# Attention: queries projected for four tiles of tokens at once, one pair of heads per bank

## The reference, cut to what matters

```python
q, k, v, g = x @ Wq, x @ Wk, x @ Wv, x @ Wg + bg        # x: 1024 x 256, W: 256 x 1024
q, k = elu(q) + 1, elu(k) + 1                           # the "features"
kv   = einsum('nd,ne->de', k, v);  k_sum = k.sum(tokens)
z    = 1 / clip(q . k_sum, 1e-6)
out  = (q * SCALE) @ kv * z * sigmoid(g)
return concat_heads(out) @ Wo                           # 1024 x 256
```

## Time and profile before

| what | value |
|---|---|
| time of three executions | 1814.41, 1815.03, 1819.37 us |
| the profiled execution | 1819.65 us, its span 1817.9 us |
| PE busy over the span | 1771.5 us, 97% |
| DVE, ACT, GpSimd busy | 1395.9, 1003.8, 528.0 us |
| between 85 and 600 us: PE, DVE, ACT busy | 510.08, 386.37, 205.76 us of 515 |

### The profile page before, as it was taken

How to read it: one execution, slowest core, us unless ns; L and a number is a source line. 1 busy time by engine, 2 the same in 40 slices (tenths; PEclk the granted TensorE clock), 3 DMA queues, 4 the chain that set the end, 5 groups by cost and what they waited for, 6 DMA issues and landing times. The chain is left out here.

```text
span 1817.9 us, 52839 instructions
## 1 busy us (share of the span) xinstructions
PE 1771.5 (97%) x19744; PEld 1554.0 (85%) x19744; DVE 1395.9 (77%) x4325; ACT 1003.8 (55%) x2481; POOL 528.0 (29%) x382
## 2 busy tenths in 40 slices
PE   8999999999999989999999999999999999989998
PEld 7879889889888778888888888888888888888887
DVE  5877877877867788888888687767888888877774
ACT  4443443443434478888887444337777777743333
POOL 0000000000000256666666000016666666611111
PEclk9999999999999999999999999999999999999999
DMA  9200000000020111111111200002111111110011
GB/s 330 83 1 2 2 1 2 1 1 2 1 72 2 40 41 29 26 29 26 29 27 35 100 12 12 1 1 70 28 27 29 27 26 29 32 35 12 6 66 33
DMA packets 64830, 60.44 MB, mean 33 GB/s; under 512 B 16415, under 2 KB 59211, under 8 KB 64718
## 3 DMA queue, kind: packets, MB, share of 16 engines
q1 hardware_dynamic: 64718, 58.88, 10.9%
HBM read 33.95 MB, written 8.39 MB: 23 GB/s over the span
## 5 line engine op out<-in xcount | busy, mean ns | idle before, releaser
L1317 ACT ACTIVATE l_probs<-l_probs,l_negmax 128x192 f32<-128x192 f32 x512 | 225.8, 442 | 86.6 <-DVE l_negmax L1424 86.6
L1142 POOL TENSOR_TENSOR l_t<-l_t,l_rnorm 128x512 f32<-128x512 f32 x128 | 136.1, 1083 | 245.5 <-DVE l_rnorm L1096 245.5
L1264 POOL TENSOR_TENSOR l_probs<-l_probs,l_rowinv 128x768 f32<-128x768 f32 x128 | 185.1, 1466 | 20.1 <-DVE l_rowinv L1453 20.1
L117 PE MATMUL ps<-local_w_hi,l_xT 128*128 128x512 f32 x384 | 158.0, 412 | 1.6 <-PEq L1719 1.1
L1272 POOL TENSOR_TENSOR l_t<-l_t,l_t 128x1024 f32<-128x1024 f32 x62 | 146.9, 2370 | 30.0 <-DVE l_t L1110 18.4
L118 PE MATMUL ps<-local_w_lo,l_xT 128*128 128x512 f32 x384 | 151.6, 395 | 0.0
L119 PE MATMUL ps<-local_w_hi,l_xT 128*128 128x512 f32 x384 | 151.3, 394 | 0.0
L117 PE MATMUL ps<-m_hnT_hi,ffn_w_hi 128*128 128x512 f32 (+1 forms) x352 | 141.0, 400 | 0.0
L512 ACT ACTIVATE attn_exp<-ps 128x512 f32<-128x512 f32 x128 | 76.4, 599 | 116.1 <-PE ps L119 116.1
L119 PE MATMUL ps<-m_hnT_hi,ffn_w_lo 128*128 128x512 f32 (+1 forms) x352 | 138.5, 394 | 0.0
L118 PE MATMUL ps<-m_hnT_lo,ffn_w_hi 128*128 128x512 f32 (+1 forms) x352 | 138.4, 393 | 0.0
(11 more groups left out here) (273 smaller groups left out, 5709.1 us busy)
## 6 DMA issues: line engine op xcount, KB each, us to landing
l_edge<-l_v SPq DMA_DIRECT2D x252, 64.0 KB, 2.0
tok_x<-x SPq DMA_DIRECT2D x16, 512.0 KB, 8.0
shifted<-x SPq DMA_DIRECT2D x64, 64.0 KB, 1.5
m_shifted<-shifted SPq DMA_DIRECT2D x16, 256.0 KB, 2.8
out<-x SPq DMA_DIRECT2D x8, 512.0 KB, 3.2
ffn_w_raw<-ffn_w SPq DMA_DIRECT2D x6, 640.0 KB
local_w_raw<-ffn_wqkv SPq DMA_DIRECT2D x4, 768.0 KB, 5.2
tok_base<-attn_base SPq DMA_DIRECT2D x4, 512.0 KB, 9.0
```

Source lines behind the costliest of these rows:

```text
L117: nc.tensor.matmul(out, wh, mh, start=start, stop=False, skip_group_check=True)
L1142: return nc.gpsimd.tensor_tensor(v, v, rn[:, a * LH:(a + 1) * LH].unsqueeze(2).to_broadcast([P, LH, DH]), ALU.mult)
L1264: nc.gpsimd.tensor_tensor(v, v, rinv[:, heads].unsqueeze(2).to_broadcast([P, LH // 2, REACH]), ALU.mult).then_inc(s.normal.sem, 1)
L1317: last = nc.scalar.activation(v, v, ACT.Exp, bias=nb[:, h:h + 1], scale=-1.0, accum_out=rsum[:, h:h + 1])
```

## The change

Queries are now projected for four tiles (512 tokens) at once. One call of `queries` for a pair of heads m fills one bank with 128 features x 512 tokens from 6 matmuls of 512 columns; before, a call filled a bank with two pairs x 256 tokens from 12 matmuls of 256 columns. Eight banks of queries are made in stage 0 for stages 0 and 1, and eight around stage 2 for stages 2 and 3. DVE writes each bank out in two instructions of 256 columns, one into `attn_qT` for the even stage, one into a new buffer for the odd stage. The order of the work in all three streams is written anew:

- PE, stage 0: after `kv_products` six banks of queries in a row (before: two), and `out_transposes` of stage 1 right after the last gates and before the third group of outputs.
- PE, stages 1 and 3: no queries ahead; `out_products` and then `out_transposes` follow each other without gates between. At the end of stage 1 the first two banks for stage 2 and 3, then `xt`, then the third bank.
- PE, stage 2: five more banks among transposes and products; `out_products` moves between the groups of outputs; `xt` is followed directly by `out_transposes` of stage 3.
- DVE and ACT follow. In stage 2, DVE does the features of banks 0 and 1, then `gated` of stage 1, third group, then the features of bank 2. In the first batch `take_kv` comes before the low part of Wo.

```diff
+    def queries_of(b, u):
+        return qt if u % 2 == 0 else qt_last if b == B - 1 else qt_key
...
+            def query_features(b, u, *pairs):
+                for m in pairs:
+                    n = AB * b + 16 + 4 * u + m
+                    dve.wait_ge(*s.attn_exp.after(n + 1))
+                    chain(nc.vector.tensor_scalar(ex[:, m % 2], ex[:, m % 2], 1.0, None, ALU.min))
...
+                    for w in range(2):
+                        cols = slice(2 * w * P, 2 * (w + 1) * P)
+                        done = nc.vector.scalar_tensor_tensor(queries_of(b, u + w)[:, m], ps[:, m % 2, cols], 0.0,
+                                                              ex[:, m % 2, cols], ALU.max, ALU.add)
+                    done.then_inc(s.attn_feat.sem, 1)
...
-                query_feature(b, 0, 0)
-                query_feature(b, 0, 1)
+                query_features(b, 0, 0, 1)
                 early.variance(nc, chain) if last else norm.variance(nc, chain)
+                take_kv(b)
                 if first:
                     dve.wait_ge(*s.attn_wo_hi.after(1))
                     nc.vector.tensor_tensor(wol[:], woraw[:], f32(woh[:]), ALU.subtract).then_inc(s.attn_wo_lo.sem, 1)
-                take_kv(b)
-                query_feature(b, 0, 2)
-                query_feature(b, 0, 3)
+                query_features(b, 0, 2, 3, 4, 5, 6, 7)
...
-            def queries(b, u, f):
...
+            def queries(b, u, *pairs):
+                for m in pairs:
+                    n = AB * b + 16 + 4 * u + m
+                    pe.wait_ge(*s.attn_feat.room(n, 2))
                     for c in range(KC):
+                        tokens = slice(2 * u * P, (2 * u + 4) * P)
+                        last = matmul3(nc, ps[:, m % 2], wh[:, Q, c, m * P:(m + 1) * P], wl[:, Q, c, m * P:(m + 1) * P],
+                                       xth[:, c, tokens], xtl[:, c, tokens], c == 0, c == KC - 1)
+                    last.then_inc(s.attn_a_full.sem, 1)
...
-                queries(b, 0, 2)
-                queries(b, 0, 3)
+                queries(b, 0, 2, 3, 4, 5, 6, 7)
...
+                for u in range(STAGES):
+                    if u == 1 or u == 3:
+                        gates(b, 2 * u, (0,))
...
+                        out_products(b, last, u, 0)
+                        out_transposes(b, last, u, 1)
+                        gates(b, 2 * u, (1,))
+                    if u == 2:
+                        queries(b, 2, 2)
+                        out_transposes(b, last, 2, 0)
+                        queries(b, 2, 3, 4)
+                        out_products(b, last, 2, 0)
+                        queries(b, 2, 5)
+                        out_transposes(b, last, 2, 1)
+                        queries(b, 2, 6, 7)
+                        gates(b, 4)
...
                     outputs(b, u, 0)
                     gates(b, 2 * u + 1, (0,))
+                    if u == 2:
+                        out_products(b, last, u, 1)
                     outputs(b, u, 1)
                     gates(b, 2 * u + 1, (1,))
...
+                    if u == 1 or u == 3:
+                        out_products(b, last, u, 1)
+                    if u == 1:
+                        queries(b, 2, 0)
+                    if not last and u == 2:
                         for w in range(2):
                             xt(b + 1, 2 * u - 2 + w)
+                    if u == 0 or u == 2:
+                        out_transposes(b, last, u + 1, 0)
+                    if not ending:
+                        outputs(b, u, 2)
+                    if u == 1:
+                        queries(b, 2, 1)
+                    if not last and u % 2:
+                        for w in range(2):
+                            xt(b + 1, 2 * u - 2 + w)
```

More of the change, by code:

```diff
@@ L593, in batch @@
                     tanh_(b, 2 * u + 1)
+                    if u == 1:
+                        exps(2, 0)
                     if last and u in (1, 2):
@@ L725, in _ @@
             early = K.tile_stats(0, EARLY)
-            def query_feature(b, u, f):
-                feature(AB * b + 16 + 4 * u + f, f, qt[:, 2 * f:2 * f + 2, :])
+            def query_features(b, u, *pairs):
[3 more added lines that the diff above has]
+                    chain(nc.vector.tensor_scalar(ex[:, m % 2], ex[:, m % 2], 1.0, None, ALU.min))
+                    if u == 0 and m == 0:
+                        dve.wait_ge(*s.attn_g_mm.after(TB * b + TB))
+                    for w in range(2):
[3 more added lines that the diff above has]
+                    done.then_inc(s.attn_feat.sem, 1)
             def batch(b, first, last):
@@ L776, in batch @@
                 for u in range(1, STAGES):
[L777 to L780, removed]
+                    if u == 2:
+                        query_features(b, 2, 0, 1)
+                        gated(b, 1, 2)
+                        query_features(b, 2, 2)
                     ot_lo(b, last, u, 0)
-                    if u > 1:
+                    if u % 2:
                         gated(b, u - 1, 2)
-                    query_feature(b, u, 2)
-                    query_feature(b, u, 3)
+                    if u == 2:
+                        query_features(b, 2, 3, 4)
                     residual(b, last, u, 0)
@@ L924, in outputs @@
                             last = nc.tensor.matmul(ps[tokens, 4 + e, at:at + OC],
-                                                    qt[r, m, which * P + half * DH:which * P + (half + 1) * DH], kv[r, m, :],
+                                                    queries_of(b, u)[r, m, which * P + half * DH:which * P + (half + 1) * DH], kv[r, m, :],
                                                     start=True, stop=True)
@@ L999, in batch @@
                 gates(b, 0)
[L1000 to L1020, removed]
+                for u in range(STAGES):
+                    if u == 1 or u == 3:
+                        gates(b, 2 * u, (0,))
+                        if first and u == 1:
+                            pe.wait_ge(*s.attn_wo_lo.after(1))
+                        out_products(b, last, u, 0)
+                        out_transposes(b, last, u, 1)
+                        gates(b, 2 * u, (1,))
+                    if u == 2:
+                        queries(b, 2, 2)
[6 more added lines that the diff above has]
+                        gates(b, 4)
+                    ending = last and u == STAGES - 1
+                    if ending:
                         x_t(0)
@@ L1024, in batch @@
                     gates(b, 2 * u + 1, (0,))
+                    if u == 2:
+                        out_products(b, last, 2, 1)
                     outputs(b, u, 1)
                     gates(b, 2 * u + 1, (1,))
-                    if last and u == STAGES - 1:
+                    if ending:
                         outputs(b, u, 2)
@@ L1030, in batch @@
                         qk(0)
[L1031 to L1034, removed]
+                    if u == 1 or u == 3:
[3 more added lines that the diff above has]
+                    if not last and u == 2:
                         for w in range(2):
                             xt(b + 1, 2 * u - 2 + w)
-                    elif u == STAGES - 1:
+                    if u == 0 or u == 2:
+                        out_transposes(b, last, u + 1, 0)
+                    if not ending:
+                        outputs(b, u, 2)
+                    if u == 1:
+                        queries(b, 2, 1)
+                    if not last and u % 2:
+                        for w in range(2):
+                            xt(b + 1, 2 * u - 2 + w)
+                    elif ending:
                         out_transposes(b, last, STAGES, 0)
```

34 lines of the change are left out of this document (18 added, 16 removed).

## The result

Four executions of the changed kernel took 1852.19, 1857.08, 1857.89 and 1858.11 us, median 1857.49. Four of the kernel before, taken beside them, had a median of 1817.2 (1814.41 to 1819.38). The ratio is 1.0214 with an interval of [1.0201, 1.0227]: slower by 40 us, where the forecast said 32. The profiled execution took 1857.89 us, its span is 1856.1, against 1817.9 before: 38.2 more.

A forecast was written before the change was run, and what follows sets the result against it. PE was taken as the bound, DVE and ACT with slack. New waits less the gain and old waits gave 8.4 + 8.2 + 8.2 + 7.6 = 32.4 us over four batches, so a median of 1847; range 1828 to 1859.

The forecast's parts named there:

- The gain: All query banks: 384 matmuls of 512 columns replace 768 of 256, 0.07 us less a bank, 4.5 us on PE's path.
- a: Six query banks in a row, stage 0, batch 1: PE waits 1.14, 0.8, and 0.2 for outputs; sum 2.1 us.
- b: Transposes of stage 1 wait for both instructions of the second `gated`, with too little PE work between: 1.15 us.
- c: End of stage 1: bank 2 of stage 2 waits for bank 0's features, behind low parts on DVE: 3.05 us.
- d: After c, bank 4 waits for bank 2's features, behind bank 1's and a `gated` on DVE: 0.65 us.
- e: End of stage 2: second tile of `xt` waits for the residual, transposes behind it for low parts; together 2.3 us.
- f: Transposes right behind products, stages 1 and 3: their second bank waits for the residual, 2 x 0.25 = 0.5 us.
- rival C: Long waits of PE, as in c in three batches, bring 1.2 GHz: +1 to +1.6 us each, 1850 to 1852; 15%.
- A: Attention part: waits stay hidden and PE's list alone counts, so faster, 1807 us; 7%.
- B: Only c and e wait as worked out, the rest comes to half: +18, 1833 us; 14%.
- D: No net change, the gain meets equal waits; would need a and b alone, in two batches, no c; 4%.
- wrong if: Signs against the forecast: a bank's features take DVE under 0.9 us, or bank 2 starts right behind `xt`.

The follow-up runs named there:

- best_narrow: The changed kernel fully reordered, but with 12 query matmuls of 256 columns a bank instead of 6 of 512: 1822.42 us, 4.3 above the same with 512.
- all_four: The changed kernel with four edits together (four query banks in stage 0; outputs, next tokens' transposes and a projection reordered): 1826.92 us, 30.6 less.

## Why the prediction was right, and where it fell short

The direction and the mechanism were right; the point, 1847, lay 10.5 us under the median. Of these, 2.2 are the kernel before, which ran at 1817.2 in this comparison; the rest is the sum, 32.4 against 40. The median lies 1.5 us above the 1838 to 1856 that were given 60%, and inside the range by 1.5. That it is inside is in part luck: the room up to 1859 had been made for the case that each half of DVE's write costs as much as the whole (+12), and the two halves took 0.75 us, as worked out. What filled the room was the clock and the other terms below.

**The gain** of 64 x 0.07 us was right (best_narrow, 4.3, or 3.2 by the batches), and the starts are 0.23 apart as in the earlier trace rows. **The return of a bank** was worked out as 2.16 us. In the rows above the bank that starts to fill at 272.74 has its last matmul at 274.00, whose slot ends at 274.23; PE starts on the same bank again at 276.34, 2.11 later. The waits below follow from that.

| term | forecast, us | measured in batches 0 to 2 |
|---|---|---|
| a, bank 4 and bank 6 of stage 0 | 1.14, 0.8 | 1.17 and 1.18, 0.73 and 0.74 (0.64 in the first) |
| a, first batch, behind the low part of Wo | 3.3 | 3.38 |
| a, outputs | 0.2 | 0.32 to 0.35 |
| b | 1.15 | 1.10 |
| c | 3.05 | 3.00 |
| d | 0.65 (its 7.15 adds up to 7.11) | 0.55 in batch 1; none in the other two, where a stretch at 1.2 GHz lies ahead of bank 4 |
| e | 1.2, 0.5, 0.6 | 1.32, 0.53, 0.44 |
| f | 2 x 0.25 | 2 x 0.24 |
| last batch: a with outputs, b | 2.4, 1.15 | 1.40 + 0.73 + 0.71, 1.10 |
| last batch, behind tables and low weights | 0.75, 0.85 | 0.69, 0.71 |
| last batch, banks of stage 2 | 0.2 + 1.9, 1.1 | 1.67, 1.08 |
| last batch, e | 1.15 | 1.11 |

**What was missing.** First, the clock: rival C had 15% and the forecast put nothing for it. It happened in part. Of three waits of c, two brought 1.2 GHz, and one wait of e as well; with an estimated 3.7 of the 6.1 us by which the four batches are over the forecast, this is the largest term that was missing. The earlier trace rows had shown such a fall after 2.06 us of wait, and the forecast's own sum made four longer ones, one of them in that very place: the likeliest case should have held one or two more. The section of the Trainium skill cited beside C would have short pauses cost too; in this profile no fall follows b, d, or a in batches 1 and 2, so for them the trace does not bear it out, but the one behind e (waits of 1.16, 0.36 and 0.28 us) does. Second, the wait of 1.17 us in the last batch: the forecast followed the copies on ACT to the exponentials and not on to the next thing queued behind them, the high part of stage 3. Third, a small one at each wait: the first matmul behind a pause holds the second off by 0.34 us and not 0.23 (272.74 to 273.08 against 273.08 to 273.31). The forecast had this only for a switch from small matmuls. Three such waits between banks of queries in batch 1 make 0.3 us. All its terms a to f together are 9.7, 0.1 under the forecast. The rest of the 0.5 by which this batch, without a fall of the clock, is over its forecast is in part the pace of the banks: in this kernel their matmuls start 0.230 us apart on average and not 0.227, 0.3 us over the 96 of a batch.

**The rivals.** A (1807, nothing waits) fell with the first row of waits. B (1833, DVE catches up during earlier waits and the rest comes to half) fell with the table above and with all_four: the waits add up. C came in part, on top of the forecast and not in place of it. D fell with c. In "wrong if", neither came: the features of a bank take DVE 0.45 + 0.75 = 1.2 us, and bank 2 starts 3.44 us behind `xt`.

## What to carry to other kernels

When work is merged into longer runs over the same two banks, compare the time that a bank takes to come back (here 2.11 us through ACT and DVE, worked out as 2.16) with the fill of the other one (1.36): every second bank more in the run pays the difference (0.73 before bank 6). Count work that is moved as cover too: the queries were worth more between transposes and products, where they hid the splits, than the 4.3 us that wide matmuls saved, and the one full reordering that was tried only came back to the start. A forecast that makes waits of 2 to 3 us on PE should hold some microseconds for the clock.

## What the runs showed of the hardware

- A matmul has a fixed part: 512 columns take 0.227 to 0.231 us from start to start and 256 take 0.119; 11 ns a matmul by the medians of the pair of kernels that differ in nothing else (8 by their batches).
- The first matmul behind a pause keeps the next one off for 0.34 us in place of 0.23.
- The clock: PE was granted 1.2 GHz after 8 of 12 waits of 3.0 us with the same work around them, over four profiles, and after 6 of 15 groups of three waits of 1.16, 0.36 and 0.28 us; with transposes of the identity in three waits of 3.0 us and one of 3.4 it kept 2.4 behind all four (one profile).
- DVE reads 256 columns of PSUM in 0.42 us and starts the next 0.34 after; two such in place of one of 512 (0.69) cost 0.07 us a bank, and in the kernel before, where DVE is idle a quarter of the time, 64 of them still showed as 1.4 us in the batches and 2.3 in the median (0.4 to 3.5).
